# Writing out a loop over batches on five engines, with constant semaphore waits instead of register waits

## The reference

```
x = x + self_attention(layernorm(x))                      # 16 heads of 16
x = x + cross_attention(layernorm(x), ctx, mask)          # 77 context tokens, 16 heads
x = x + soft_moe(layernorm(x))                            # 8 experts x 128 slots

soft_moe: xn = rms_norm(x) * gamma;  logits = xn @ slots^T            # 256 x 1024
          dispatch = softmax over tokens; combine = softmax over slots
          h = gelu((dispatch^T xn) @ w1) @ w2;  out = combine @ h
```

## Time and profile before

| | us |
|---|---|
| median of 3 runs (2017.63 to 2021.10) | 2020.74 |
| the profiled execution | 2018.85 |
| its span, first to last instruction | 2017.0 |
| PE busy | 1812.1 (90%) |
| DVE, ACT, POOL busy | 1081.9, 961.5, 418.7 |
| mean granted TensorE clock | 0.947 of full speed |

### The profile page before, as it was taken

How to read it: one execution, slowest core, us unless ns; L and a number is a source line. 1 busy time by engine, 2 the same in 40 slices (tenths; PEclk the granted TensorE clock), 3 DMA queues, 4 the chain that set the end, 5 groups by cost and what they waited for, 6 DMA issues and landing times.

```text
span 2017.0 us, 41529 instructions
## 1 busy us (share of the span) xinstructions
PE 1812.1 (90%) x16912; PEld 1596.0 (79%) x16912; DVE 1081.9 (54%) x2224; ACT 961.5 (48%) x1688; POOL 418.7 (21%) x349
## 2 busy tenths in 40 slices
PE   2566799999999999999999999999999999998876
PEld 1343688889888888888888888888888888888866
DVE  4333456556565555556565656556565656554422
ACT  2211354555555464555545464555545464555442
POOL 1000111222212221222221222122221222122222
PEclk7565799999999999999999999999999999999889
DMA  4000000000000000000000000000000000000000
GB/s 142 1 8 1 8 1 7 9 7 9 1 15 1 15 1 9 7 7 9 2 14 1 15 1 10 7 7 9 2 14 1 15 2 9 7 1 6 1 6 6
DMA packets 20851, 19.88 MB, mean 10 GB/s; under 512 B 9921, under 2 KB 19777, under 8 KB 20289
## 3 DMA queue, kind: packets, MB, share of 16 engines
q1 hardware_dynamic: 20672, 17.06, 2.9%
HBM read 12.86 MB, written 4.19 MB: 8 GB/s over the span
## 4 chain that ended last, share of the span: by engine, by line
PE 81%; DVE 9%; issue 4%; ACT 3%; SPq 1%; POOL 1%; DMA 0%; POOLq 0%; DVEq 0%; ACTq 0%
PE ps L347 19%; PE ps L348 17%; PE ps L349 17%; PE ps L432 4%; PE ps L469 3%; PE ps L563 2%; PE ps L609 2%; PE ps L647 2%; PE ps L579 1%; PE ps L452 1%; PE ps L544 1%; PE ps L499 1%; PE ps L638 1%; PE ps L389 1%; DVE sl_lo L900 1%
## 5 line engine op out<-in xcount | busy, mean ns | idle before, releaser
L1238 POOL TENSOR_TENSOR h_lo<-h_f,h_hi 128x512 fp32r<-128x512 f32 x256 | 330.4, 1291 | 1186.0 <-DVE h_hi L1110 1186.0
L347 PE MATMUL ps<-w_hi,h_hi 128*128 128x256 f32 x1024 | 304.9, 298 | 32.7 <-issue 22.2
L347 PE MATMUL ps<-sl_hi,w_hi 128*128 128x256 f32 x1024 | 304.2, 297 | 22.0 <-DVE cb_lo L900 21.6
L348 PE MATMUL ps<-w_hi,h_lo 128*128 128x256 f32 x1024 | 292.1, 285 | 0.0
L349 PE MATMUL ps<-w_lo,h_hi 128*128 128x256 f32 x1024 | 292.0, 285 | 0.0
L348 PE MATMUL ps<-sl_hi,w_lo 128*128 128x256 f32 x1024 | 290.8, 284 | 0.0
L349 PE MATMUL ps<-sl_lo,w_hi 128*128 128x256 f32 x1024 | 290.7, 284 | 0.0
L1110 DVE CAST h_hi<-h_f 128x512 fp32r<-128x512 f32 x256 | 132.2, 516 | 241.0 <-ACT h_f L860 240.9
L347 PEld LDWEIGHTS ps<-w_hi,h_hi 128*128 128x128 f32 x1024 | 198.2, 194 | 62.5 <-issue 51.1
L977 DVE TENSOR_REDUCE mx<-ps 128x8 f32<-128x2048 f32 x64 | 146.4, 2288 | 151.9 <-PE ps L432 151.9
L860 ACT ACTIVATE h_f<-ps 128x512 f32<-128x512 f32 x256 | 152.4, 596 | 156.5 <-PE ps L349 156.0
(11 more groups left out here) (193 smaller groups left out, 4141.5 us busy)
## 6 DMA issues: line engine op xcount, KB each, us to landing
x<-in_x SPq DMA_DIRECT2D x16, 256.0 KB, 2.7
out<-acc SPq DMA_DIRECT2D x16, 256.0 KB, 2.2
g_w<-in_w SPq DMA_DIRECT2D x2, 1024.0 KB, 6.1
cx<-in_ctxT SPq DMA_DIRECT2D x16, 77.0 KB, 2.0
g_wqk<-in_wqk SPq DMA_DIRECT2D x1, 1024.0 KB, 6.9
g_se<-in_se SPq DMA_DIRECT2D x1, 1024.0 KB, 9.6
biases<-in_bias SPq DMA_DIRECT2D x1, 640.0 KB, 4.9
mk_i<-in_mask SPq DMA_DIRECT2D x16, 38.5 KB
```

Source lines behind the costliest of these rows:

```text
L347: te.matmul(o, lhs[0], rhs[0], start=first, stop=False)
L348: te.matmul(o, lhs[1], rhs[0], start=False, stop=False)
L1238: Q_.tensor_tensor(h_lo[:, part, :], h_f[:, part, :], h_hi[:, part, :].bitcast(f32), ALU.subtract)\
```

## The change

Both hardware loops become Python loops, so that the stages are written out in the instruction streams of all five engines and every wait and every DMA address is a constant.

```diff
@@ -168,7 +168,7 @@
     run(engine, steps, FIRST, c=0, s=0)
     run(engine, steps, c=1, d=0)
     run(engine, steps, c=2, d=1, m=0)
-    with handle.Fori(1, B - 2) as b:
+    for b in range(1, B - 2):
         run(engine, steps, c=b + 2, d=b + 1, m=b, l=b - 1)
     run(engine, steps, d=B - 1, m=B - 2, l=B - 3)
     run(engine, steps, LAST, m=B - 1, l=B - 2)
@@ -1320,7 +1320,7 @@
             load_x(2)
             load_ctx(2)
             load_x(3)
-            with sp.Fori(1, B - 3) as b:
+            for b in range(1, B - 3):
                 load_ctx(b + 2)
                 store(b - 1)
                 load_x(b + 3)
```

## The result

| | before | after |
|---|---|---|
| median, us | 2019.18 (4 runs, 2016.23 to 2021.10) | 1995.57 (4 runs, 1995.38 to 1997.21) |
| ratio | | 0.9886, 95% interval 0.9869 to 0.9903 |
| span of the first profile, us | 2017.0 | 1993.6 |
| all runs of these two kernels, later ones too: median | 2017.6 (43 runs, 2009.05 to 2022.58) | 1996.5 (10 runs, 1994.78 to 1998.93) |

The change is faster, by 23.6 us in the first comparison and by 21.1 over all runs. The forecast was 2001.0 with a range of 1997.0 to 2004.5: right in direction and in where the gain comes from, 5.4 us too high, and just outside its range.

What follows compares the result with a forecast made beforehand. PE was taken as the bound, 1812.1 us busy of 2017.0. From the profiled 2018.85 us came off 18.0 for twelve stages and 0.1 for stage 1, other terms zero: 2000.8, said as 2001.0, range 1997.0 to 2004.5.

Steps and rivals of the forecast that it cites:

- The branch on PE: At the loop's twelve branches back: PE's gaps of 1.60 to 2.22 us go, then PE waits for DVE's xh_d.
- the twin: Stage 1, entered by falling into the loop, with full work: 111.39 us, and a 0.26 us wait for xh_d.
- The period: Length of a written-out stage, read from stage 1 x1 to x1: between 111.45 and 111.60 us, taken as 111.5.
- the term of 18.0: Gain over the twelve branched-into stages: 1356.02 - 12 x 111.5 = 18.0 us.
- Registers, the other engines' branches, SP, their code: Register work, DVE, ACT and POOL branches, SP's DMA queue, and at most 60 more code packets: each taken as zero.
- The fetch of a block as a rival: After lt at the turn: a late code page, not the branch, causes the stall, which stays; 2017 to 2019 us, 3%.
- The first rival: At the turns: all 22.2 us of PE's idle time comes back, registers may cost too; 1996.7 or 1992.7 us, 7%.
- The drop of the clock: In stage 12: 3.41 us at 1.2 GHz, costing 1.7 us, counted as gone; if it stays, the gain is 16.4.
- The sum: Whole kernel: the profiled 2018.85 us less 18.1 gives 2000.8, said as 2001.0; 2002.7 if the median's surplus stays.
- shorter runs: Whole kernel: with the period of 111.45, the reason given for the forecast's lower end of 1999 us.

Runs made afterwards that it cites:

- slot0: Kernel before with all loops and registers kept, PE's loop body moved to the start of a 256-instruction fetch block; 2000.21 us, ratio 0.9914.
- hint: Kernel before with loops and registers kept, PE's loop announcing its branch back at its head (`hint_back_edge=True`); 1996.61 us, ratio 0.9902.
- others_only: Kernel before with DVE, ACT, POOL and SP written out, PE keeping its hardware loop; 2014.22 us, ratio 0.9995.
- pe_only: Kernel before with only PE's loop written out, DVE, ACT, POOL and SP keeping theirs; 1996.71 us, ratio 0.9897.
- xt_late: Changed kernel with PE's transposes of xh_d moved after outer for e=1; 2047.69 us, 1.0154 of the kernel before.
- slot224: Kernel before with PE's loop body placed at slot 224 of its 256-instruction fetch block, loops and registers kept; 1999.74 us, ratio 0.9912.

## Why the prediction was right or wrong

- **The branch on PE: right.** The cause, the place, the number (twelve) and what is late next are as told: PE waits 0.27 us for xh_d at each turn (7.6 us, 15 times, of which 3.9 is one early wait), where the twin had 0.26.
- **The period: right within 0.08.** 111.5 was forecast; 111.58 is the mean of the first profile's twelve stages, 111.56 that of all four profiles. DVE's line gained what it was to gain: in the changed kernel xh_d's transposes start 4.31 us after x1 (446.85 - 442.54), in the twin 4.44. But the matmuls up to xh_a's transposes then took 3.38 us (450.23 - 446.85) against 3.34 (341.79 - 338.45), and further hundredths went by later. slot0 and hint, with registers, have 111.51 and 111.49, so the constant waits are if anything 0.05 to 0.09 slower; why was not tried. Against the profile it was read from, the term of 18.0 measured 17.1, and stage 1 gave nothing (111.39 to 111.46) in place of 0.1.
- **Registers, the other engines' branches, SP, their code: right, zero.** others_only stands at 0.9995 of the kernel before (0.9982 to 1.0007). A middle of a stage took 50.70 us in stage 0 and 50.73 in the changed kernel's stage 2 (467.21 to 517.94). q14 carried 27 packets more (40 against 13), not up to 60, and no stage shows them, except perhaps 0.1 us in stage 7 (111.69): each of the four profiles has one such stage, of 111.67 to 111.69, and pe_only, where the others keep their loops, has none (111.53 to 111.57).
- **The fetch of a block as a rival**: the point "the gap stands three matmuls behind the branch's target, so the branch itself had been passed" was read rightly and weighed wrongly. I gave it to the rival that nothing would change; it was the key to the mechanism, and slot0 shows that a stage need not be written out at all. By the rule of the Trainium skill's page "Runtime: NRT & Kernel Launch" ("Instruction fetch mechanics") that I cited (prefetch only forward), a straight line has no such gap; the trace agrees: the row of 22.2 us is gone from the changed kernel. The compare-and-branch of about 108 ns that the Trainium skill's page "Advanced Engine Details and Errata" ("Control Flow Timing") gives holds for no taken branch of PE here: 3.3 to 3.9 us unannounced, 0.36 to 0.49 announced.
- **The first rival: refuted, though its number came nearest.** "All of the idle time comes back" gave 1996.7 us, and 1995.57 was measured. That is luck. Of the 22.2 us of gaps in the profile before, the loop gave back 17.1, and PE waits for xh_d at each turn as the forecast said; the rest of the 23.3 us lay outside the loop, where the rival changes nothing.
- **The drop of the clock: right in cause, too small.** I counted one drop as gone. All profiles together tell it better: 1, 3, 2 and 4 drops in the four profiles of before, 2 in others_only, 9 in xt_late with its 2.75 us waits, none in these stages of the four of after, of pe_only, slot0, hint and slot224, whose gaps at the turn are at most 1.4 us. The first profile was the mildest of four: its loop took 3.8 us less than their mean, so the 18.1 us counted as gain were 21.0 for the mean of four profiles.
- **The sum: here it failed.** The failed step is the base from which the gain was taken. The step "The profiled execution took 2018.85 us", with all outside the loop carried over unchanged, took one draw for the value. That profile had 549.5 us outside the loop, 4.7 above the mean of four; the changed kernel has 544.3 on average. The 5.2 us between are nearly all of the miss of 5.4: with 544.3 in place of 549.5 the forecast would have been 1995.8. The two chance parts of that profile lay on opposite sides (4.7 long outside, 3.8 short inside), so its time stood close to the median and looked typical. Counted against the mean kernel and not against this one profile, the same failure stands in the gain: 18.1 us where the loop gives 21.0. The prediction saw the spread of 3.5 us among the runs, but put it on top of the forecast (2002.7), and below it only as "shorter runs", down to 1999.
- **The range**: its lower end, 1997.0, left 4 us for a draw that is lower, the clock's share outside the loop included; four profiles of one kernel there span 10.0 us.

## What to carry to other kernels

A stage or turn that the kernel already runs without the suspected cost, here the loop's first stage, prices a change better than the idle row does: in the profile that was forecast from, 22.2 us of idle time were worth 17.1. Before writing a loop out, look where PE's gap stands behind the branch: if it is a few instructions in, moving the body to the start of a fetch block or announcing the branch gives the same time in the loop with a small program (over whole executions only the announced branch was shown to match, 1996.61 against 1996.5; slot0 had 2000.21). And where a forecast carries stretches over unchanged, compare their granted clock with what other executions could have: a profile is one draw, and two deviations can cancel in its total.

## What the runs showed of the hardware

- PE's code comes in blocks of 256 instructions: 135 packets of 16 KB on q8 for the 34,691 PE instructions in the trace of the straight program. After an unannounced branch back, two blocks were fetched one behind the other. The branch took 3.3 to 3.9 us, and the first matmul behind the gap started 2.9 to 3.7 us after its end. PE's queue of matmuls covered the first, and the second only if enough work stood before it.
- Single gaps in otherwise full stretches at 2.4 GHz: in the five profiles with the 12 gaps in place (the four of before and others_only, 1.40 to 2.44 us each), 12 of the 60 were followed by 3.4 us at 1.2 GHz, which cost 1.5 to 1.7 us. All 12 stood behind gaps of 1.90 us or more, as 23 without a drop did; the 25 shorter gaps, and the 12 of 0.8 to 1.4 us in slot224, had none. Of the twelve turns with a wait of 2.75 us in xt_late, nine had it.
- Outside the loop, where PE waits much, the clock rose and fell at other places in each execution of the same program: from 60 to 120 us it was 0.53 of full speed in the first profile of before and 0.66 in the second. The whole stretch took 549.5 and 539.6 us there.
